# Perceiver block on one core: the first unit's key rows loaded straight from SBUF, the mask flag summed earlier, and the two branch bodies exchanged

## The reference, cut to what matters

```python
# x: (2,128,128), source ctx: (2,2048,128), bias: (2,1,128,2048), all zeros in this input
q = einsum('bfd,dnh->bfnh', layernorm(x), wq) * 8 ** -0.5
k = einsum('btd,dnh->btnh', ctx, wk)
v = einsum('btd,dnh->btnh', ctx, wv)
logits = einsum('btnh,bfnh->bnft', k, q) + bias
x = x + einsum('bnft,btnh,nhd->bfd', softmax(logits), v, wo)
```

## Time and profile before

| | us |
|---|---|
| Median of 3 runs | 333.61 (333.51 to 333.70) |
| The profiled execution's own time | 331.68 |
| Its span on the engines | 329.7 |
| PE busy | 285.2 (87%) |
| DVE busy | 231.8 (70%) |
| ACT busy | 206.7 (63%) |
| Granted TensorE clock, mean | 0.928 of full |

### The profile page before, as it was taken

One profiled execution on the slowest core, in us unless ns is written; L12 is line 12 of the kernel. 1 busy time (PEld: TensorE's weight loads), 2 busy tenths in 40 slices (PEclk: granted clock), 3 DMA queues, 4 the chain that ended last, 5 costly groups with the idle time before them and its releaser, 6 DMA issues.

```text
span 329.7 us, 10086 instructions
## 1 busy us (share of the span) xinstructions
PE 285.2 (87%) x4246; PEld 186.9 (57%) x4246; DVE 231.8 (70%) x374; ACT 206.7 (63%) x423; POOL 71.5 (22%) x136
## 2 busy tenths in 40 slices
PE   7847999999999997889648899999999984894886
PEld 5334566667676644735315566767666653342655
DVE  5935899999999835363556899999999803714572
ACT  4572698988989872324402698988989870251141
POOL 5792500000000025220360630000000000300033
PEclk9996999999999998799965999999999995899599
DMA  7943325522224505220000025422231000000000
GB/s 256 414 158 116 126 74 203 174 76 79 72 88 126 213 2 191 95 89 12 0 0 0 2 75 175 165 75 84 66 90 60 3 2 0 2 2 0 0 2 16
DMA packets 10688, 27.84 MB, mean 84 GB/s; under 512 B 2209, under 2 KB 3169, under 8 KB 10258
## 3 DMA queue, kind: packets, MB, share of 16 engines
q1 hardware_dynamic: 10568, 26.97, 24.4%
q10 hardware_dynamic: 74, 0.20, 0.2%
HBM read 20.74 MB, written 6.42 MB: 82 GB/s over the span
## 4 chain that ended last, share of the span: by engine, by line
PE 69%; DVE 14%; issue 8%; ACT 3%; DMA 3%; POOL 2%; SPq 1%; DVEq 0%; POOLq 0%
PE bank L932 67%; DVE mx L698 4%; DVE s_neg L767 1%; DMA k_scratch<-kparts 1%; DMA kpair<-k_scratch 1%; DVE kparts L668 1%; POOL y L324 1%; DVE xn L656 1%; DVE k_rest L665 1%; PE bank L1152 1%; PE bank L963 1%; ACT probs L470 0%; ACT xnT L423 0%; DVE v_all L758 0%; SPq L236 0%
## 5 line engine op out<-in xcount | busy, mean ns | idle before, releaser
L698 DVE TENSOR_REDUCE mx<-bank 128x2 f32<-128x1024 f32 x128 | 154.4, 1224 | 21.7 <-PE bank L932 18.0
L470 ACT ACTIVATE probs<-bank 128x512 f32<-128x512 f32 x256 | 139.4, 595 | 18.2 <-PE bank L932 14.0
L932 PE MATMUL bank<-q_exp,kpair 64*128 64x128 bf16 x1024 | 84.9, 217 | 1.3 <-ACT probs L470 0.5
L932 PE MATMUL bank<-kpair,q_rows 64*128 64x512 bf16 x256 | 74.6, 394 | 8.6 <-DMA kpair<-k_scratch 7.1
L932 PE MATMUL bank<-probs,v_all 128*9 128x128 f32 x2048 | 79.9, 274 | 1.1 <-ACT probs L470 1.0
L932 PEld LDWEIGHTS bank<-q_exp,kpair 64*128 64x128 bf16 x1024 | 55.7, 94 | 31.6 <-issue 15.0
L932 PEld LDWEIGHTS bank<-probs,v_all 128*9 128x9 f32 x2048 | 43.2, 90 | 15.3 <-ACT probs L470 4.0
L361 POOL CAST m_rows<-negm 128x2 bf16<-128x2 f32 x32 | 6.2, 193 | 154.4 <-DVE negm L705 154.4
L932 PEld LDWEIGHTS bank<-kpair,q_rows 64*128 64x128 bf16 x256 | 22.7, 94 | 10.4 <-issue 7.8
L423 ACT ACTIVATE v_all<-bank 128x512 f32<-128x512 f32 (+1 forms) x18 | 10.1, 575 | 23.8 <-PE bank L932 23.8
L324 POOL TENSOR_TENSOR y<-ve,mhalf 128x2 f32<-128x2 f32 x6 | 4.2, 695 | 54.1 <-DVE ve L647 54.1
(11 more groups left out here) (209 smaller groups left out, 348.9 us busy)
## 6 DMA issues: line engine op xcount, KB each, us to landing
k_scratch<-kparts SPq DMA_DIRECT2D x24, 256.0 KB, 2.9
kpair<-k_scratch SPq DMA_DIRECT2D x63, 96.0 KB
kpair<-k_scratch SPq DMA_DIRECT2D x63, 64.0 KB
ctxT_s<-in_ctxT SPq DMA_DIRECT2D x4, 512.0 KB, 6.6
mask_s<-in_mask SPq DMA_DIRECT2D x2, 1024.0 KB, 10.7
kpair<-k_scratch SPq DMA_DIRECT2D x63, 32.0 KB
wM<-in_packM SPq DMA_DIRECT2D x1, 1728.0 KB, 7.1
wB<-in_packB SPq DMA_DIRECT2D x1, 727.0 KB, 6.4
```

The lines of the kernel that those rows point to most:

```text
L470: act.activation(probs[:, j % 4, :], bank[:, 4 + j % 2, :], ACT.Exp).then_inc(S("exp_done"), 1)
L698: V.tensor_reduce(mx[n % 2][:, w, :], bank[:, 2 * (w % 2):2 * (w % 2) + 2, :], AX.X, ALU.max) \
L932: return T.matmul(out_, lhsT=lhsT, rhs=rhs, start=start, stop=stop, **kw)
```

## The change

Unit 0's rows are no longer read back from the scratch but copied from `kparts` itself, in SBUF, by a new function, and both halves are issued earlier: head 0 on SP right behind the stores, no longer after their landing; head 1 on ACT ahead of mask 1's sum. DVE makes the flag before its two query pieces. The condition is reversed, so that the body without masks is placed first, directly behind the branch, and the body with masks between it and the continuation.

```diff
+        def first_head(eng, a):
+            for kp in range(PARTS):
+                times = K_TIMES[kp]
+                row = a * HOFF + K_BASE[kp]
+                src = kparts[a * HD:(a + 1) * HD, kp, 0:SK].unsqueeze(1).to_broadcast([HD, times, SK])
+                eng.dma_start(kpair[0][row:row + times * HD, :], src).then_inc(S("k_loaded0"), 16)
...
+            sp.wait_ge(S("k_ones"), U)
+            first_head(sp, 0)
             sp.wait_ge(S("k_stored0"), 16 * 2 * PARTS)
-            sp.wait_ge(S("k_ones"), U)
-            load_head(sp, 0, 0, 0, 0, 0)
...
             for i in range(4):
                 stage_k(0, i)
+            act.wait_ge(S("k_ones"), U)
+            act.wait_ge(S("k_low"), 4)
+            first_head(act, 1)
             act.wait_ge(S("in_mask1"), 16)
...
             for c in range(V_EARLY[0]):
                 prep_v(0, c)
-            act.wait_ge(S("k_stored0"), 16 * 2 * PARTS)
-            act.wait_ge(S("k_ones"), U)
-            load_head(act, 0, 0, 0, 0, 1)
             cross(0)
...
-            for k in range(2, 4):
-                put_rows(0, k)
             dve.wait_ge(S("mask1_sum"), 1)
...
             V.tensor_copy(flag_i[:, :], bank[0:1, 7, 0:1]).then_inc(S("flag"), 1)
+            for k in range(2, 4):
+                put_rows(0, k)
...
-            with pe.If(entries > 0):
+            with pe.If(entries < 1):
+                cross(0, False)
+            with pe.Else():
                 cross(0, True)
-            with pe.Else():
-                cross(0, False)
```

## The result

| | before | after |
|---|---|---|
| Median of 20 runs each, same chip, us | 332.81 (330.62 to 334.17) | 334.86 (332.54 to 336.37) |
| Profiled execution's own time, us | 331.68 | 334.04 |
| Its span, us | 329.7 | 332.1 |
| Granted TensorE clock, mean | 0.928 | 0.923 |

Ratio after to before 1.0066 [1.0042, 1.0090]: the change makes the kernel slower by about 2.1 us (1.4 to 3.0). The forecast of 329.8 had the wrong sign, and the median lies above its range of 328.0 to 332.1.

A forecast was written before the change was run, and what follows sets the result against it. PE's 7.1 us wait for unit 0's key rows, sent through HBM, was taken to bound the start. A gain of 4.1 less 0.3 for the jump gave 3.8: 333.6 - 3.8 = 329.8 us, range 328.0 to 332.1.

The forecast's parts named there:

- The jump at the end: End of the body: the jump now passes 1401 rows; cost taken as 0.3 us, between 0 and 2.5.
- Rival B: End of the body: the jump is exposed and costs 1.8 to 2.5 us, giving 331.3 to 332.0; chance 16%.
- Key rows: Start: without the scratch round trip, unit 0's last key rows land at 22.8 us, bounds 21.3 and 29.1.
- Rival C: Start held later than 23.5 by slow flag reading or SBUF loads, leaving 1.5 to 2.3 us gain; chance 9%.
- Rival E: Start: head 0's 48 rows come one at a time, PE starts at 28.7, total 335.6 us; chance 5%.
- What stands on ACT: ACT before the branch: three issues take 1.99 us, mask's sum starts at 17.2, third value tile at 21.7.
- The branch: Start: target follows directly, PE through at 22.4, 0.7 us after the third tile; the turn is worth 2.6.
- PE's gain at the start: First cross-attention: PE starts at 22.9 against 26.98, a gain of 4.1 us.
- the flag edit: DVE before the branch: flag made ahead of two query pieces, worth 0.
- unit 1's keys: Behind the start: unit 1's keys land at 27.2 to 29.2 against 28.9 wanted; hidden or up to 0.3 late.
- the distance inside the body: From PE's start to the last output product, 99.8 us before: to stay within 1 us, apart from the clock.
- The clock: Half-clock stretches around PE's idle time: up to 1.5 us more gained, or similar size either way; taken as 0.

The follow-up runs named there:

- run 1: Before with only the branch condition reversed and the two bodies exchanged; ratio to before 1.0074.
- run 3: After with the body that adds the masks replaced by one small matmul, so the jump passes almost nothing; ratio to before 0.9923.
- run 9: After with PE's program up to its wait for `comb` written into both bodies and the jump to the common rest there; ratio to before 0.9899.
- run 2: After with the branch bodies back in their old order; ratio to before 1.0050.
- Run 4: Before with unit 0's six loads in their old places but reading `kparts` in SBUF; ratio to before 1.0058.
- run 7: After with PE's whole continuation in both bodies and head 0's SBUF copies ahead of the second half's stores; ratio to before 0.9963.
- run 10: After with head 0's SBUF copies ahead of the second half's stores and the join moved to the wait for `comb`; ratio to before 0.9923.
- run 5: After with PE's whole continuation written into both bodies, so no join behind them; ratio to before 1.0006.
- run 12: Before with only the flag made ahead of DVE's two pieces of query rows; ratio to before 1.0012.
- run 6: Before with the branch turned and PE's whole continuation in both bodies, keys still through the scratch; ratio to before 1.0033.
- run 8: Before, turned, continuation in both bodies, first two heads' rows stored to the scratch separately and loaded once these land; ratio to before 0.9970.

## Why the prediction was wrong

Two terms of the sum failed, by 2.5 and 2.9 us, and either alone would have left a gain of about 1 us. The wrong sign needs both.

**The first step that failed is "The jump at the end", and its "I take 0.3".** It measured 2.8 (2.84 in after, 2.76 in run 1, 0.04 in runs 3 and 9). I had argued that the idle array before the last groups gives PE's sequencer time to run ahead to the jump. It doesn't get there: it reads the jump only as the last output product starts (125.70 in after, 127.34 in run 1), and that product had itself waited for ACT's `o_sb`. It does run ahead over matmuls that wait for nothing, as run 9 shows. Rival B, at 16%, was the right mechanism, and still too cheap at 1.8. It counted 2.2 until the fetch starts and 0.9 for the page, and nothing behind the landing; the runs show 1.01 to 1.56 to its start, 0.95 to 1.42 for it, and 1.56 more until PE runs. The 2.2 was misread: it is the distance from the landing of one page to the start of the next, which is 2.1 to 2.5 in after and in runs 1 and 2 too, while PE is already at work. The branch of before was read at 21.88, its page started 1.8 later, and it was over 1.5 after the landing. From the last output product to the next matmul it is 4.0, in all of which only 1.23 is covered, by the product itself, `o_rec` and `onorm`. The rule of the Trainium skill (page "Runtime: NRT & Kernel Launch", section "Instruction fetch mechanics") that a taken branch out of the prefetched window stops execution for a fetch is what the trace shows at 127.26 to 128.21; I named it and gave it too little.

**The second is "Key rows", a term of the wrong size.** I had the last rows landed at 22.8; they came at 25.64. I took the issue time (0.69) and the landing (4.40) of loads from HBM, since no row had a source of 8 partitions. The last copy was issued at 21.13, not 18.4: the stores' issues took 1.2 more, and the copies' 1.51 each. Its landing took 4.51, as I had it. Run 4 shows the source by itself to be slow. Rival C (the start held by slow loads or a slow flag, 9%) was this mechanism. B and C each left a gain; I had no rival in which they come together. Rival E's 335.6 lies close by luck: it had the 48 rows come one at a time, but although a row took 0.40 engine-us (19 / 48) instead of 0.21, ACT's 48 ran within 16.9 to 21.8 us in after, about four at once. The page "SBUF — State Buffer" (section "Door 1: The DMA port swizzle") of the Trainium skill had led me to an estimate of 3.5 us for a head's 192 KB and 21.9 for the landing; that it is the ports, no run here shows.

**"What stands on ACT"**: the same term again. The three issues took 3.21 instead of 1.99 (3.2 to 4.6 over the runs), the mask's sum started at 17.76, not 17.2, the third tile was there at 22.19, not 21.7. Hidden behind the late keys in after; in runs 7 and 10, whose keys are earlier, it sets the start. The two edits collide here: ACT pays in front of PE's branch for rows that were to come early.

**"The branch"**: that the turn takes the branch out of the start is right (no page in 19.75 to 25.78, and the branch takes 0.09 instead of the 3.88 of run 2). That it is worth 2.6 held only against the start that I forecast: in before the branch was over at 26.06, ahead of the keys. Both its prices were low: 1.37 for reading the flag, not 0.7, and 5.36 in all instead of 3.8. And the first is no constant. The flag loads in 0.48 in nine traces, but in 0.69 to 1.90 in after and runs 2, 4, 5 and 9, all of which load it while copies out of `kparts` are under way (as does run 3, though, in 0.48, 1 us before its last rows land). So with earlier keys after could have started at 24.81 + 0.17 = 24.98 in this execution, and at 22.19 + 1.37 = 23.56 with a flag loaded as in run 7. PE's gain at the start was 1.2, of 4.1 forecast, 0.5 of it the early front.

**Right**: the flag edit is worth 0 (run 12, made on before); unit 1's keys stay hidden in after (its first scores at 33.30, with PE at work before); the distance inside the body; and what was to show me wrong did: keys after 23.5, and the gap at the jump grown by over 0.5.

**The clock** was taken at 0. The stretch to `s_neg` is 15.2 in the eight traces with 6.8 us of half clock there, 16.1 to 16.5 in the five with 10.2, after among them, and 17.51 in run 1 with 17.1. So the +0.9 of after is the clock's. Whether the gap brings it is left open: four of the five have no gap, and one of the two with the gap has the longest stretch of all. The granted clock over all executions points to the gap, 0.9165 in run 1 (10 executions) against 0.9234 in before beside it (22), a loss of 0.0069, of which 2.8 us of idleness at half clock are 2.8 x 0.5 / 335 = 0.0042. Taking the jump away is worth 5.6 us by the ratios (1.0066 against 0.9899) and 4.1 by the medians (334.86 for after, 330.73 for run 9, on different chips), more than the gap; a longer slow stretch would account for about 1 of it, and the interval of run 9 alone is 1.4 us to each side.

## What to carry to other kernels

Before a branch is turned, list every place where either path leaves straight-line code and ask at each what PE has still to do there. Exposed, a far jump costs 4.0 us on this kernel from the last matmul before it to the first behind it. It is free where PE's array has that much work in hand whose matmuls wait for nothing (here the 16 in front of the wait for `comb`); an array idle for want of data doesn't help, because the sequencer stands at the same wait. A shorter path for data isn't a faster one: find a row with the same source shape, or allow for an issue that blocks its engine for 2 us behind a slow transfer, and ask whose engine makes the issue. When a term has bounds of 0 and 2.5 and no row between them, don't put the value near the end you like. And when two rivals each fall short of turning the sign, price them together.

## What was unexpected of the hardware

- Copies out of `kparts` on 8 partitions (48 rows of 4 KB per head): 19 engine-us a head in after and 18 in run 4 with no store beside them, against 10 out of the scratch. ACT's third issue takes 1.6 to 2.9 us instead of 0.5, while its first two stay within 0.2 of before's in after.
- PE's load of the flag from SBUF takes 0.48 us in nine traces and 0.69 to 1.90 in five, all of them beside such copies.
- A far branch holds PE's sequencer for 3.3 to 5.2 us, a near one for 0.09 to 0.19. PE runs only 1.56 (after and run 1) and 1.63 (run 2) after the page of instructions has landed.
- The sequencer reads a jump 6.4 us before the array has finished the 16 matmuls in front of it (run 9), but not before a wait in front of it ends.
- A far jump at the very end of PE's program goes with a longer execution at the same span: a median of 3.2 to 3.3 us between own time and span in runs 5 to 8 (44 executions), 1.93 to 2.02 in all other kernels.
